# The last context layer's image prepared beside the experts of two earlier layers, its attention in one stage for each of two rounds

## The reference, cut to what matters

```
def bitnet_linear(x, W, b):
    w_scale = maximum(mean(abs(W)), 1e-5)
    qW = sign(W) * (abs(W) > 0.5 * w_scale)
    i_scale = maximum(max(abs(x)), 1e-8) / 127      # over the WHOLE tensor
    qx = clip(round(x / i_scale), -128, 127)
    return qx @ qW.T * (w_scale * i_scale) + b

vis = bitnet_linear(dinov2_features, W_d2v, b_d2v)    # the context: 4 x 1601 x 96 -> 128
image_embeds = bitnet_linear(vis, W_img, b_img)       # 4 x 1601 x 128
fused = bitnet_linear(text_embeddings, W_txt, b_txt)  # needs x
for Wa, ba in ((W_att0, b_att0), (W_att1, b_att1)):
    kv = bitnet_linear(image_embeds, Wa, ba)          # 64 wide, k = [kv, kv]
    attn = softmax(fused @ k.T / sqrt(128))
    fused = fused + 0.1 * attn @ k
avg_img = mean(image_embeds, axis=1)
h = relu(bitnet_linear(concat(fused, avg_img), W_f1, b_f1))
out = bitnet_linear(h, W_f2, b_f2)
```

## Time and profile before

| | |
|---|---|
| median of 3 runs | 5240.53 us (5238.18 to 5243.85) |
| the profiled execution's own time | 5234.44 us |
| its span, first to last instruction | 5232.7 us |
| PE, DVE, ACT, POOL busy | 72%, 61%, 35%, 6% of the span |
| mean granted TensorE clock | 0.832 of full speed |

### The profile page before, as it was taken

How to read it: one execution, slowest core, us unless ns; L and a number is a source line. 1 busy time by engine, 2 the same in 40 slices (tenths; PEclk the granted TensorE clock), 3 DMA queues, 4 the chain that set the end, 5 groups by cost and what they waited for, 6 DMA issues and landing times. The chain is left out here.

```text
span 5232.7 us, 55928 instructions
## 1 busy us (share of the span) xinstructions
PE 3747.6 (72%) x22064; PEld 2030.3 (39%) x22068; DVE 3171.1 (61%) x4441; ACT 1835.7 (35%) x1976; POOL 299.4 (6%) x143
## 2 busy tenths in 40 slices
PE   4699999999999345777667607665457948167579
PEld 2444444444444132333355404222234636134256
DVE  4466666666666664898744475999734252642442
ACT  1255555555555122444313212444213313022123
POOL 1000000000000001000000011444100000000000
PEclk8899999999999676999879856666668868578689
DMA  2000000000000001000010010000010010100100
GB/s 67 2 0 0 0 0 1 1 0 0 0 0 1 7 18 19 7 7 7 17 62 1 2 47 1 0 0 0 0 44 1 1 38 1 29 0 0 40 1 5
DMA packets 12879, 56.17 MB, mean 11 GB/s; under 512 B 2081, under 2 KB 2593, under 8 KB 11970
## 3 DMA queue, kind: packets, MB, share of 16 engines
q1 hardware_dynamic: 12626, 52.70, 3.3%
HBM read 48.89 MB, written 0.52 MB: 9 GB/s over the span
## 5 line engine op out<-in xcount | busy, mean ns | idle before, releaser
L923 PE MATMUL banks<-L0x_q_context,L0x_context 96*128 96x512 f32 (+1 forms) x1632 | 742.0, 596 | 10.0 <-ACT L0x_ring L1017 9.3
L948 PE MATMUL banks<-L0x_ring,L0x_context_rows 128*97 128x512 f32 (+1 forms) x1632 | 737.5, 594 | 1.1 <-ACT L0x_ring L1003 1.1
L1017 ACT COPY L0x_ring<-banks 128x1024 f32<-128x1024 f32 (+1 forms) x416 | 413.0, 995 | 658.5 <-PE banks L923 658.5
L1067 DVE TENSOR_TENSOR L0x_maxima<-L0x_maxima,L0x_ring 128x1024 f32<-128x1024 f32 (+1 forms) x288 | 342.6, 1194 | 257.2 <-ACT L0x_ring L1017 256.1
L1048 DVE TENSOR_TENSOR L0x_ring<-L0x_ring,L0x_spread 128x2048 f32<-128x2048 f32 (+1 forms) x208 | 457.2, 2200 | 18.4 <-ACT L0x_spread L991 18.4
L923 PEld LDWEIGHTS banks<-L0x_q_context,L0x_context 96*128 96x128 f32 (+1 forms) x1632 | 300.1, 188 | 396.8 <-issue 378.1
L948 PEld LDWEIGHTS banks<-L0x_ring,L0x_context_rows 128*97 128x97 f32 (+1 forms) x1632 | 262.0, 164 | 416.8 <-issue 413.7
L1003 ACT ACTIVATE L0x_ring<-L0x_ring 128x2048 f32<-128x2048 f32 (+1 forms) x208 | 384.0, 1847 | 11.4 <-DVE L0x_ring L1048 11.4
L1423 ACT ACTIVATE L1x_probs<-banks 128x2048 f32<-128x2048 f32 (+1 forms) x112 | 196.6, 1755 | 267.9 <-PE banks L1354 225.9
L1456 DVE TENSOR_REDUCE L1x_maxima<-banks 128x3 f32<-128x1203 f32 (+1 forms) x176 | 241.6, 1373 | 69.5 <-PE banks L1323 69.5
L1323 PE MATMUL banks<-L1x_k,L1x_q 32*128 32x401 f32 x1024 | 179.2, 584 | 118.6 <-DVE L1x_maxima L1456 102.0
(11 more groups left out here) (957 smaller groups left out, 5884.1 us busy)
## 6 DMA issues: line engine op xcount, KB each, us to landing
L1f_expert_weights<-in_L1f_experts SPq DMA_DIRECT2D x16, 512.0 KB, 9.6
L2f_expert_weights<-in_L2f_experts SPq DMA_DIRECT2D x8, 512.0 KB, 6.9
L3a_expert_weights<-in_L3a_experts SPq DMA_DIRECT2D x8, 512.0 KB, 6.5
L3f_expert_weights<-in_L3f_experts SPq DMA_DIRECT2D x8, 512.0 KB, 6.4
L1x_k<-L1x_k_rows SPq DMA_DIRECT2D x64, 50.0 KB
L0x_context_rows<-in_context_rows SPq DMA_DIRECT2D x1, 2448.0 KB, 27.7
L0x_context<-in_context SPq DMA_DIRECT2D x1, 2401.5 KB, 19.0
L1x_context<-in_context SPq DMA_DIRECT2D x4, 600.4 KB, 5.6
```

The lines of the kernel that those rows point to most:

```text
L923: mm = pe.matmul(k.ps[0:height(j), i, :], c1[:, j * P:j * P + height(j)], q1[:, u // 2 % 2, :], start=True, stop=True)
L948: mm = pe.matmul(k.ps[0:CW, bank, :], rows1[0:height(j), j, :], ring[0:height(j), s % RING, i, :], start=s == FIRST[u] and i == 0, stop=s ...
L1017: act.copy(ring[0:r, s % RING, 2 * p:2 * p + len(pair), :], k.ps[0:r, 2 * p:2 * p + len(pair), :]).then_inc(copied, 1)
L1067: dve.tensor_tensor(o, before, ring[0:r, s % RING, 2 * p:2 * p + m, :], ALU.max).then_inc(maxed, 1)
```

## The change

The context, the weights and the rows of L3_xattn are loaded in a stage at the start of `layer2_ffn`. Everything of the preparation runs inside the `experts` stages of L2_ffn (`ImageFirst`: ternary weights, first and second integers, first projection, three of the four batches of the second) and of L3_attn (`ImageLast`: the last batch, the mean, the third integers), as generators that `experts` advances: PE one small matmul after each of its row tiles, ACT and DVE one step for each half of an expert. To free two PSUM banks for it, the two rings of `experts` go from four banks to three, in all three layers that call it (L3_ffn is handed `Nothing`). Keys and values of all batches and both rounds come from one new stage, `project_image`, and `attend_image` becomes one stage for each round, with four batches interleaved; the loop is gone. Rounding loses one pass (ACT scales, DVE rounds in one), the ternary weights two operations for each, and the clipping to -128 and 127 goes.

```diff
-def experts(k, name, a, xT, gates, acc, b1, func):
+def experts(k, name, a, xT, gates, acc, b1, func, beside):
+    U = 3
@@ tensor @@
-                        if n >= 4:
-                            pe.wait_ge(activated, n - 3)
+                        if n >= U:
+                            pe.wait_ge(activated, n - U + 1)
...
                         mm.then_inc(product, 1)
+                        next(other, None)
@@ scalar @@
                 for e in range(E):
                     for half in range(2):
+                        if e:
+                            next(other, None)
@@ vector @@
+                        if t % 4 == 3:
+                            next(other, None)
...
+class ImageAhead:
...
+                sp.dma_start(self.big[0:CD, :].rearrange("c (b n) -> c b n", b=B), k.dram["context"].rearrange("b c n -> c b n")).then_inc(self.here, 16)
+                sp.dma_start(w[:], k.dram["L3_xattn_weights"]).then_inc(self.here, 16)
+                sp.dma_start(r[:], k.dram["L3_xattn_rows"].broadcast_to([P, length])).then_inc(self.here, 16)
...
+class ImageFirst(ImageWork):
+    def tensor(self, pe):
+        n = 0
+        for h in range(16):
+            for c in range(4):
+                q, b = (0, h - 5) if h < 10 else (1, h - 13)
+                if 0 <= b < B:
+                    if c == 0:
+                        pe.wait_ge(self.rounded, B * q + b + 1)
+                    if h == 5 and c == 0:
+                        pe.wait_ge(self.halved, 2)
+                    self.multiply(pe, q, b, c, n)
+                    n += 1
+                yield
+    def scalar(self, act):
+        n = 0
+        for h in range(16):
+            for q in range(2):
+                if h in (3 + 8 * q, 4 + 8 * q):
+                    act.wait_ge(self.scaled, q + 1)
+                    self.divide(act, q, 2 * (h - 3 - 8 * q))
+                    self.divide(act, q, 2 * (h - 3 - 8 * q) + 1)
+            q, b = (0, h - 5) if h < 10 else (1, h - 13)
+            if 0 <= b < B:
+                for c in range(4):
+                    self.take(act, q, b, c, n)
+                    n += 1
+            yield
...
+def project_image(k, ints, attn, joint, biases, rows, keys, v):
+            for n, (i, b) in enumerate(units):
+                for half in range(2):
+                    if n:
+                        pe.wait_ge(kept, 2 * n - 1 + half)
+                    for c, m in CHUNKS[2 * half:2 * half + 2]:
+                        mm = pe.matmul(k.ps[0:64, c // 512, 0:m], attn[i][:, 0:64], ints[:, b * CTX + c:b * CTX + c + m], start=True, stop=True)
+                    mm.then_inc(filled, 1)
+                for half in range(2):
+                    if n >= 2:
+                        pe.wait_ge(taken, 2 * n - 3 + half)
+                    for j in range(8 * half, min(8 * half + 8, JT)):
...
+                    act.activation(keys[0:64, i, b, c:c + m], k.ps[0:64, 2 * half:2 * half + 2, :].rearrange("p a n -> p (a n)")[:, 0:m],
+                                   ACT.Identity, bias=biases[i][0:64], scale=joint[0:64, 2 + i:3 + i]).then_inc(kept, 1)
...
+def attend_image(k, halves, qT, keys, v, fused, bufs):
...
+            for b in range(B):
+                more = b + 1 < B
+                if more:
+                    scan(b + 1, 0, 3)
+                add(b, 0)
+                score(b, 2)
+                if more:
+                    scan(b + 1, 3, 6)
+                add(b, 1)
+                score(b, 3)
+                if more:
+                    scan(b + 1, 6, M)
+                if b:
+                    set_upright(b - 1)
+                add(b, 2)
+                if more:
+                    turn(b + 1)
+                add(b, 3)
+                if more:
+                    score(b + 1, 0)
+                    score(b + 1, 1)
+            set_upright(B - 1)
...
@@ layer2_ffn @@
+    k.image_ahead = image = ImageAhead(k)
     with ExitStack() as ctx:
         w = load_weights(k, "L2_ffn", ctx)
...
+                sp.wait_ge(image.here, 48)
+        experts(k, "L2f", ew, k.zT, gates, acc, w["b1"], ACT.Relu, ImageFirst(image))
@@ layer3_context @@
             for i in range(2):
                 to_columns(k, fused, k.zT)
-                with k.loop(B) as b:
...
+                attend_image(k, halves, k.zT, keys[:, i], v[:, i], fused, bufs)
```

554 lines of the change are left out of this document (372 added, 182 removed).

## The result

The changed kernel takes 5086.35 us (median of 4 executions, 5083.64 to 5089.4), against 5239.35 us for the kernel before in the same comparison (5234.19 to 5243.85): a ratio of 0.9709, with a 95% interval of 0.9697 to 0.9722. The forecast was 5086.0. The agreement to 0.4 us is luck, as the account behind the experiments shows. The rest of this document compares the traces.

What follows compares the result with a forecast made beforehand. Stages end in barriers, each bounded by its longest chain (PE in experts, DVE in preparation). Terms -106 + 16 + 0.5 + 6 + 7 + 1 - 79 = -154.5 us give 5086 from the median 5240.53; range 5066 to 5118, upper end carried to 5130.

Steps and rivals of the forecast that it cites:

- The preparation on the path: Ahead of the text's normalisation: 128.2 us go, memsets and `project_image` take 22 instead; -106 us, ends -110 and -87.
- The loads: In SP's queue: context, weights and rows stand ahead of L2_ffn's own weights, which the next stage awaits; +16 us.
- the library: GpSimd in L3_attn: a new library instruction ahead of the IOTA, with nothing else running; +6 us, ends 6 and 12.
- The experts: PE's added image matmuls: +7 us in L2_ffn's experts, +1 in L3_attn's; everything else hides in PE's time.
- The first rival: Cover in the experts too thin: added ACT and DVE work comes on the path, half being 66 us, 5150; chance 0.13.
- The attention: Last context layer's two rounds: 251 us become twice 86, -79 us; ends -107 and -44.
- The first batch's scans come alone, at first at 1.2 GHz: Start of each attention round: first batch's scans take 8.8 us, 14.7 with query, maxima, turn and placing.
- the prediction's own test: Attention rounds: granted clock over 0.93 would show the forecast; below 0.9 would make the prediction wrong.
- The second rival: Clock does not hold in the rounds: scans' two-bank ring causes short PE waits, half at 1.2 GHz, 5161; chance 0.09.

Runs made afterwards that it cites:

- kernel with the three edits: Changed kernel with image loads and memsets moved to L2_ffn's convolution stage, L3_attn's IOTA behind L2_ffn's experts' all-reduces, and scans and scores on 128 rows: 5040.13 us.
- places_ahead: Changed kernel with L3_attn's IOTA moved behind the last all-reduce of L2_ffn's experts stage and its own stage removed: 5081.83 us.
- run warm: Changed kernel with useless bf16 matmuls on PE where it waits anyway (16, 22, 4 and 6 at a place): 5085.24 us, ratio 0.9707.

## Why the prediction was right, and where it was not

**The preparation on the path** (-106, measured -109). `project_image` was put between 16 us (ACT alone) and 39 (PE at 1.2 GHz), and I took 20; it took 17.4, with ACT's sixteen evictions at 15.34 busy. The choice near ACT's end was right for the reason given: the clock came back at 4504.7, five us into the stage.

**The loads** (+16, measured +14.2) and **the library** (+6, measured +7.0) were right in mechanism and size, and moving each off the path gave the time back (all of it in the kernel with the three edits). The estimate from the earlier trace rows counted the context's share as 11.3 us; it landed 13.7 us after its issue, but the two loads behind it followed within 3.0 us where the sum had 4.7. The Trainium skill (GPSIMD Engine Reference, "Instruction dispatch") gives approximately 6 us for the first call to a freshly loaded kernel, with no visible instruction; the traces agree in kind and show 6.9 us here from the library instruction (4255.1) to the IOTA (4262.0), and 7.1 in the run places_ahead.

**The experts** (+7 and +1, measured +5.2 and, from L3_attn's first expert matmul to DVE's last addition, +0.7: 114.7 to 115.4). PE alone pays, 0.75 us for four matmuls instead of 1.0. The evictions with a sum cost ACT a further 0.19 us instruction each, which the sum of ACT's half had not, and it changed nothing. The first rival (cover too thin) is excluded for this kernel and has its place shown: with 28 more evictions the stage is 6.5 us longer.

**The attention** (-79, measured -63.2) is the term that was mis-sized, by 16 us. The step that failed is "*The first batch's scans come alone, at first at 1.2 GHz*", with the clock at full speed behind them. It was sized from the earlier trace rows, where the clock was back at 4627.6, 10 us into the batch and within its first scans. The changed kernel's round 1 reached the full clock only 33 us after its query began. The rounds spent 63.5 us at 1.2 GHz. By the prediction's own test (granted over 0.93, wrong below 0.9) its claim on the clock was wrong: 0.82 and 0.86. The second rival named the right quantity and the wrong cause and size. It had half of each round at 1.2 GHz, +75 us, from short waits at the banks; it came to a third, +16, and PE was busy 27.87 of the 30 us at the head of round 1.

The cause is the edit that I did not cost at all: scans on 64 rows of the array instead of 128. Instructions and columns stay, and one instruction takes the same at the same clock (eight scan instructions at 2.4 GHz 3.20 us in the run warm, 3.21 with 128 rows), so a sum of times per instruction shows no difference. Two opposite edits show it: 128 rows in the changed kernel cut the low time from 63.5 to 15.8 us and the rounds by 27.3, and 64 rows in the kernel before raised it from 85.0 to 245.5 and the rounds by 69.5. The Trainium skill (TensorE: Matmul & The Clock Gate, "What's actually happening") has the throttle released by how busy PE is, with no part for rows; by that rule the clock would have come back early in the scans of round 1, and in the changed kernel's trace it did not, with PE busy 27.87 of 30 us. The Trainium skill's section "A second HAM failure mode: psum-queue depth-cycling" (same page) would have the scans' turn through two banks as the cause: four banks left round 1's 36.2 us unchanged, and 128 rows with two banks cut them to 9.0. Whether the scans' 64 rows or the scores' 65 weigh more was not separated, since each edit changed both, and by what mechanism rows act on the clock is not shown.

With 128 rows the rounds are 166.6 us against the 178 that the forecast comes to with the turning of `fused`. The forecast's terms were read from instructions with 128 rows, so this is the like comparison, and its order of work was 11 us too high: at the start of a round (13.7 us from the query to the first score, 14.7 taken) and in the batches (17.8 instead of 11.5 + 5.7 + 1.7 = 18.9, since most of the waits between batches never came). That a batch with 64 rows took 18.8, the forecast's figure, is chance. So the 16 us are the difference of two errors: rows cost 27 that were not counted, and 11 were counted that did not come.

The hit to 0.4 us is luck. The attention's gain was 15.8 us too large; the other terms and the rest of the span came out 7.1 better than forecast, which leaves the sum 8.7 too large against the traces. Of that the two profiled executions hide 7.1, as they lie on opposite sides of their medians, and another 1.2 is the median of the kernel before, 5239.35 where the forecast started from 5240.53.

## What to carry to other kernels

Work that moved beside a stage bound by PE cost what it put on PE and nothing else, as long as ACT and DVE had room in their halves; but its loads, library changes and small stages must be moved too, to a place where their queue is free: here all 21 us of them came back so. When an edit shrinks operands to the rows in use, look at the granted clock and not only at durations per instruction: zero rows that bring a matmul back to 128 cost PE nothing and gave 27 us of the rounds, 25.5 of the kernel. Where few rows can't be helped, matmuls on 128 rows between them held the clock up here. Read a matmul that only keeps the clock up as work with a price: six of them held up the first scan. Compare traces by stretches between named operations when single executions differ by as much as the effect.
